# The sixteen batches of a cross attention: written out in line instead of a loop of two a turn

## The chip, the cores and the metric

The kernel runs on one core of a Trainium2 chip. The metric is the device time of one execution in microseconds, and a run is compared by its median. TensorE (PE), VectorE (DVE), ScalarE (ACT), GpSimd (POOL) and SyncE (SP) each run their own list of instructions; they meet only through semaphores.

## What is computed

A decoder layer on 16 batches of 100 tokens of width 128, in float32: a banded self attention, a cross attention with 16 heads over 1444 context rows per batch, and a mixture of 16 experts plus a shared part.

```python
x = x + _L0_attn_ref(_layernorm(x), WQ, WK, WV)
x = x + _L0_xattn_ref(_layernorm(x), ctx_1024, ctx_1024, mask, W_Q, b_Q, W_K, b_K, W_V, b_V, W_out, b_out)
x = x + _L0_ffn_ref(_layernorm(x), Wg, W1, b1, ...)
# _L0_xattn_ref, for each batch and head:
scores = jnp.einsum('bhqd,bhkd->bhqk', Q, K) / np.sqrt(D_K)
scores = jnp.where(attn_mask[:, None, :, :], -10000.0, scores)
attn = jax.nn.softmax(scores, axis=-1)
out = jnp.einsum('bhqk,bhkd->bhqd', attn, V)     # then @ W_out.T + b_out
```

## The kernel before

`decoder` runs three stages one after the other: `self_attention` (to about 112 us of the span), `cross_attention`, and `experts` (from about 1418 us). The cross attention is the subject. Weights are folded beforehand, so that a query row of a head is taken straight against the context, and products in float32 are made of three matmuls on operands split in a high and a low part (`_hi`, `_lo`).

A batch is one period of work. Its 1600 rows (100 tokens by 16 heads) are 12 tiles of 128 rows and one of 64. For each tile TensorE makes two halves of the scores (`score`, L1082), DVE adds the mask's bias and keeps the row's least (L997), ACT takes the exponential (L934), POOL normalizes by `row_inv` (L875, L877). TensorE then turns the rows (`turn`, transposes of L1098), ACT and DVE copy them out of PSUM as `pT_hi` (L943) and `pT_lo` (L1012), and TensorE multiplies them by the context (`values`, L1128), three steps behind the transposes. Each period also carries the preparation of the next batch (`prep`, context and queries) and, at 0.41 of its length, the projection of the batch before (`project`, L1171 to L1175), which DVE adds to the residual at L1059, once for each batch.

The order inside a period is a list, `ORDER`, worked out by `period()` on the host; each engine walks its own sorted form of it in `emit(b, odd)`. `odd` selects one of two sets of buffers, so two periods differ in buffers only. All engines share `periods`, which calls `emit` for -1, 0, 15 and 16 with a constant batch number, and for 1 to 14 in a loop of each engine, two batches a turn: seven turns, six jumps back. With a constant number every wait is against a constant, and one that is always met is left out; in the loop, `b` is in a register, each threshold is computed by the engine, and `wait_apart` adds a count on a semaphore of its own (`passed_sp`, `passed_pool`, `passed_dve`) behind the wait. `periods` is called in the blocks of all five engines. In the loop TensorE has 594 matmuls for each batch, and the other engines 140 (DVE), 86 (ACT) and 58 (POOL) instructions that do work.

Of the kernel before, what the change touches and what calls it, by code (L numbers as in the profile page):

```python
# [16 lines left out]
NB, S, D = 16, 100, 128  # L17
# [642 lines left out]
def cross_attention(nc, ctx_in, mask, banks, ident, A_hi, A_lo, VO, u, c_all,  # L660
# [3 lines left out]
    with ExitStack() as ctx:  # L664
# [84 lines left out]
        def periods(engine, emit):  # L749


            emit(-1, 1)
            emit(0, 0)
            with engine.Fori(1, NB - 2, 2) as b:
                emit(b, 1)
                emit(b + 1, 0)
            emit(NB - 1, 1)
            emit(NB, 0)

        with nc.Block() as block:  # L760
            @block.sync
            def _(sp):
# [37 lines left out]
                def emit(b, odd):  # L800
# [12 lines left out]
                    if here(b, 0) and here(b, 1):  # L813
# [3 lines left out]
                        load_x1(b + 1, 1 - odd)  # L817

                periods(sp, emit)
                sp.wait_ge(x2_stored, 16 * NB)  # L820

            @block.gpsimd
            def _(pool):
# [93 lines left out]

                start()
                periods(pool, emit)

            @block.scalar
            def _(act):
                order = act_order()

                def emit(b, odd):
                    for _, kind, db, j in order:
# [23 lines left out]
                        elif kind == "prep":  # L950
# [9 lines left out]
                            else:  # L960
# [3 lines left out]
                                act.copy(dst, qf[n % 2][:, :, :]).then_inc(prep_hi, 1)  # L964

                periods(act, emit)

            @block.vector
# [897 lines left out]
```

## Time and profile before

| | |
|---|---|
| median of 3 runs | 1603.62 us (1602.78 to 1609.25) |
| the profiled execution | 1606.2 us |
| its span, first to last instruction | 1604.5 us |
| busy: PE, DVE, POOL, ACT | 91%, 71%, 61%, 55% |
| mean granted clock of TensorE | 0.951 |
| matmuls | 10557 |
| first and last projection added (DVE L1059) | 240.12, 1415.71 us |

Busy shares are means over three unlike stages. "Idle before" in the timeline is the time an engine stood still ahead of a piece of work, and what ended it, as far as the semaphores show; "issue" means that nothing it waited for is seen. The granted clock is a share of TensorE's full speed.

### The profile page before, as it was taken

The numbers are of one execution on the slowest core, as the hardware profiler recorded it, in microseconds if no ns is written. First come the engines' busy times: TensorE is split into PE (matmuls) and PEld (weight loads), VectorE is DVE, ScalarE is ACT, GpSimd is POOL, SyncE is SP. The second block draws the span as 40 slices with busy tenths as digits, with TensorE's granted clock in tenths as the row PEclk, the third lists the DMA queues.
The fourth block names the chain that finished last, engine by engine and source line by source line (L and its number), as shares of the span: only waits on it lengthen the run. The fifth ranks groups of instructions, "written<-read, shape, count | busy, mean of one in ns | idle before, by whom it ended". The sixth has DMA issues, their size and how long they took to land. (4 is left out here: it accounts for less than half of the span.)

```text
span 1604.5 us, 35506 instructions
## 1 busy us (share of the span) xinstructions
PE 1463.2 (91%) x10557; PEld 1408.8 (88%) x10557; DVE 1143.5 (71%) x2672; ACT 883.8 (55%) x1632; POOL 973.1 (61%) x1101
## 2 busy tenths in 40 slices
PE   4856999999999999999999999999999999956796
PEld 4736999999999999999999999999999999945585
DVE  5644878686878687868686868686868686768565
ACT  0303656565656565656565656565656565625453
POOL 2015858575857585757675767576757585414564
PEclk9956999999999999999999999999999999966898
DMA  7021111111111111111110111011101011024422
GB/s 164 1 68 62 54 34 52 35 50 35 52 35 50 35 52 35 50 36 50 35 55 31 52 34 55 31 54 32 55 31 55 30 33 35 8 65 113 113 61 88
DMA packets 98038, 80.76 MB, mean 50 GB/s; under 512 B 17577, under 2 KB 96530, under 8 KB 97714
## 3 DMA queue, kind: packets, MB, share of 16 engines
q1 hardware_dynamic: 88848, 71.83, 15.1%
q10 hardware_dynamic: 6882, 2.21, 1.0%
q0 software_dynamic: 2112, 4.29, 0.8%
q8 instruction: 101, 1.65, 0.4%
q14 instruction: 95, 0.78, 0.1%
HBM read 67.26 MB, written 11.04 MB: 49 GB/s over the span
## 5 line engine op out<-in xcount | busy, mean ns | idle before, releaser
L943 ACT CAST pT_hi<-banks 128x512 fp32r<-128x512 f32 (+1 forms) x672 | 360.9, 542 | 342.6 <-PE banks L1098 337.5
L1012 DVE TENSOR_TENSOR pT_lo<-banks,pT_hi 128x512 fp32r<-128x512 f32 (+1 forms) x576 | 358.2, 626 | 220.3 <-ACT pT_hi L943 212.4
L875 POOL TENSOR_SCALAR probs<-probs,row_inv 128x1408 f32<-128x1408 f32 x192 | 278.7, 1451 | 235.7 <-DVE row_inv L1004 235.4
L1098 PE MATMUL banks<-ident,probs 128*128 128x128 f32 (+1 forms) x2304 | 365.8, 274 | 5.3 <-POOL probs_half L877 3.2
L1128 PE MATMUL banks<-pT_hi,ctx_hi 128*128 128x256 f32 (+1 forms) x1056 | 329.5, 312 | 17.8 <-DVE pT_lo L1012 13.8
L863 POOL TENSOR_SCALAR bias<-mask,c_cur 128x1444 f32<-128x1444 uint8 x192 | 282.9, 1473 | 82.4 <-DVE nmax L997 64.3
L934 ACT ACTIVATE probs<-probs,nmax 128x1448 f32<-128x1448 f32 x192 | 289.8, 1509 | 39.0 <-DVE nmax L997 38.9
L1128 PE MATMUL banks<-pT_hi,ctx_lo 128*128 128x256 f32 (+1 forms) x1056 | 303.1, 287 | 0.0
L1128 PE MATMUL banks<-pT_lo,ctx_hi 128*128 128x256 f32 (+1 forms) x1056 | 302.4, 286 | 0.0
L1098 PEld LDWEIGHTS banks<-ident,probs 128*128 128x128 f32 (+1 forms) x2304 | 271.0, 140 | 17.0 <-DVE pT_lo L1012 9.0
L1082 PE MATMUL banks<-ctxT_hi,qh 128*128 128x362 f32 x832 | 241.9, 372 | 4.8 <-POOL ql L912 2.8
L1128 PEld LDWEIGHTS banks<-pT_hi,ctx_hi 128*128 128x128 f32 x1056 | 201.1, 190 | 23.7 <-issue 16.0
L1082 PE MATMUL banks<-ctxT_lo,qh 128*128 128x362 f32 x832 | 208.2, 332 | 0.0
L1082 PE MATMUL banks<-ctxT_hi,ql 128*128 128x362 f32 x832 | 207.8, 331 | 0.0
L1128 PEld LDWEIGHTS banks<-pT_lo,ctx_hi 128*128 128x128 f32 x1056 | 200.8, 190 | 0.0
L1128 PEld LDWEIGHTS banks<-pT_hi,ctx_lo 128*128 128x128 f32 x1056 | 200.2, 190 | 0.0
L997 DVE CUSTOM_DVE_ANT_0 probs<-banks,bias,nmax 128x724 f32<-128x724 f32 x192 | 185.1, 964 | 4.6 <-PE banks L1082 3.9
L997 DVE CUSTOM_DVE_ANT_0 probs<-banks,bias 128x724 f32<-128x724 f32 x192 | 173.9, 906 | 12.8 <-PE banks L1082 7.6
L1082 PEld LDWEIGHTS banks<-ctxT_lo,qh 128*128 128x128 f32 x832 | 150.4, 192 | 0.0
L1082 PEld LDWEIGHTS banks<-ctxT_hi,ql 128*128 128x128 f32 x832 | 149.8, 191 | 0.0
L1082 PEld LDWEIGHTS banks<-ctxT_hi,qh 128*128 128x128 f32 x832 | 127.4, 193 | 8.0 <-DVE nmax L997 4.7
L964 ACT CAST qh<-qf 128x200 fp32r<-128x200 f32 x128 | 70.2, 548 | 104.7 <-DVE qf L1052 104.7
(287 smaller groups left out, 2339.9 us busy)
## 6 DMA issues: line engine op xcount, KB each, us to landing
mask<-in_mask_BxSxS_bk SPq DMA_DIRECT2D x192, 180.5 KB
nat<-in_ctx SPq DMA_DIRECT2D x16, 704.0 KB
up_raw<-in_L_ffn_W SPq DMA_DIRECT2D x32, 128.0 KB, 2.7
xs_dram<-empty SPq DMA_DIRECT2D x1, 2600.0 KB, 8.2
rows<-xs_dram SPq DMA_DIRECT2D x10, 260.0 KB, 3.0
down_raw<-in_L_ffn_W SPq DMA_DIRECT2D x16, 128.0 KB, 3.1
t_both<-yk_dram SPq DMA_DIRECT2D x3, 512.0 KB, 5.3
mask_half<-in_mask_BxSxS_bk SPq DMA_DIRECT2D x16, 90.2 KB
```

What stands on the lines that cost most here:

```text
L863: pool.tensor_scalar(bias[(t + i) % 2][0:n, 0:SK], src[:, :], MASKED, c_cur[i][0:n, t:t + 1], ALU.mult, ALU.add).then_inc(bias_ready, 1)
L875: pool.tensor_scalar(prob(j)[0:n, 0:FIRST], prob(j)[0:n, 0:FIRST], rinv[0:n, s:s + 1], 1.0, ALU.mult, ALU.mult)
L934: act.activation(prob(j)[0:n, 0:SKP], prob(j)[0:n, 0:SKP], ACT.Exp, bias=nmax[0:n, 1, s:s + 1], scale=-1.0, accum_out=rsum[0:n, s:s + 1]). ...
L943: act.copy(pT_hi[tslot(i, j)][:, 0:w], banks[:, T_BANK + j % 2, 0:w]).then_inc(turned_hi, 1)
L964: act.copy(dst, qf[n % 2][:, :, :]).then_inc(prep_hi, 1)
L997: dve.tensor_tensor_reduce(prob(t)[0:n, cs].rearrange("p (a k) -> p a k", a=2), src, bias[(t + i) % 2][0:n, cs].rearrange("p (a k) -> p a ...
L1012: dve.tensor_tensor(p_lo, turn, p_hi.bitcast(F32), ALU.subtract).then_inc(turned_lo, 1)
L1082: last = pe.matmul(banks[:, S_BANK + c, 0:CW], qpart[:, rows], kpart[:, c * CW:(c + 1) * CW], start=first, stop=qpart is ql[i])
L1098: last = pe.transpose(banks[0:m, T_BANK + j % 2, at_col:at_col + 128], prob(t)[:, c0:c0 + m], ident[:, :])
L1128: last = pe.matmul(banks[:, out_bank(g), 0:w], stationary[:, k, :], moving[tslot(i, j)][:, cs], start=(k == 0 and stationary is ctx_hi[i] ...
```

## The change

The six lines of `periods` become one loop on the host, which writes every batch out with a constant number. The same periods come in the same order with the same buffers: `b % 2` is 1 for -1 and 15 and 0 for 0 and 16, as in the calls it takes the place of.

```diff
@@ -749,13 +749,8 @@
         def periods(engine, emit):
 
 
-            emit(-1, 1)
-            emit(0, 0)
-            with engine.Fori(1, NB - 2, 2) as b:
-                emit(b, 1)
-                emit(b + 1, 0)
-            emit(NB - 1, 1)
-            emit(NB, 0)
+            for b in range(-1, NB + 1):
+                emit(b, b % 2)
 
         with nc.Block() as block:
             @block.sync
```

What follows from it in code that isn't edited: `known(b)` is now true for every batch, so `wait` and `wait_apart` take their constant form throughout, DMA sources are fixed slices in place of `bass.ds(b, 1)`, and the semaphores `passed_...` are never counted. Each engine's program holds sixteen periods where it held two and the four calls around them.

## Rows read from the trace of the kernel before

**Rows 1.** The page: span, busy time of the engines, TensorE's slices and granted clock.
```profile
span 1604.5 us, 35506 instructions
PE 1463.2 (91%) x10557; PEld 1408.8 (88%) x10557; DVE 1143.5 (71%) x2672; ACT 883.8 (55%) x1632; POOL 973.1 (61%) x1101
...
PE   4856999999999999999999999999999999956796
...
PEclk9956999999999999999999999999999999966898
```

**Rows 2.** The page: queues that carry only instructions.
```profile
q8 instruction: 101, 1.65, 0.4%
q14 instruction: 95, 0.78, 0.1%
```

**Rows 3.** Who waited for whom, TensorE: engine line waited for: us, times, longest.
```profile
PEld banks L1128 <- issue: 16.0, 7, 2.7
...
PE banks L1128 <- DVE pT_lo L1012: 13.8, 6, 2.4
```

**Rows 4.** Timeline 838.9 to 845.7: start, us, work [idle before <-releaser].
```profile
841.03 0.60 PE L1098 MATMUL banks<-ident,probs 128*128 128x128 f32 x4
...
842.52 0.68 DVE L1012 TENSOR_TENSOR pT_lo<-banks,pT_hi 128x512 fp32r<-128x512 f32 x1
...
842.82 1.47 POOL L863 TENSOR_SCALAR bias<-mask,c_cur 128x1444 f32<-128x1444 uint8 x1
843.99 0.19 PEld L1128 LDWEIGHTS banks<-pT_hi,ctx_hi 128*128 128x128 f32 x1 [2.59 <-issue]
844.00 0.38 PE L1128 MATMUL banks<-pT_hi,ctx_hi 128*128 128x256 f32 x1 [2.36 <-DVE pT_lo L1012]
...
845.47 0.42 DVE L1023 TENSOR_TENSOR oT_lo<-banks,oT_hi 128x256 fp32r<-128x256 f32 x1 [2.27 <-issue]
```

**Rows 5.** Busy time, stretches between projections: us, busy, clock, DMA.
```profile
core 0: us, PE busy (x) PEld busy (x) DVE busy (x) ACT busy (x) POOL busy (x), PEclk, DMA share, GB/s
318.52:399.91 81.39, 79.01 (x594) 77.76 (x594) 59.77 (x140) 48.46 (x86) 54.44 (x58) 0.98 0.14 43
...
478.34:559.96 81.62, 78.99 (x594) 77.76 (x594) 59.78 (x140) 48.47 (x86) 54.37 (x58) 0.98 0.14 42
559.96:638.35 78.39, 77.81 (x594) 76.41 (x594) 59.51 (x141) 48.33 (x86) 54.47 (x58) 1.00 0.14 43
638.35:718.49 80.14, 77.48 (x594) 76.25 (x594) 59.68 (x140) 48.49 (x86) 54.41 (x58) 1.00 0.14 43
718.49:796.88 78.39, 77.81 (x594) 76.39 (x594) 59.51 (x140) 48.36 (x86) 54.55 (x58) 1.00 0.14 44
796.88:878.51 81.63, 79.03 (x594) 77.79 (x594) 59.77 (x140) 48.48 (x86) 54.41 (x58) 0.98 0.14 42
...
1198.31:1276.68 78.37, 77.77 (x594) 76.36 (x594) 59.51 (x140) 48.33 (x86) 54.49 (x58) 1.00 0.14 43
1276.68:1354.66 77.98, 77.56 (x593) 76.19 (x593) 59.54 (x141) 48.34 (x86) 54.61 (x58) 1.00 0.10 33
```

**Rows 6.** The same view, the stretch after one stop.
```profile
844.31:847.72 3.41, 3.41 (x16) 3.41 (x15) 1.11 (x2) 0.58 (x1) 0.00 (x0) 0.50 0.20 59
```

**Rows 7.** Timeline of TensorE, two changes of batch without a jump.
```profile
1249.93 0.43 PE L1098 MATMUL banks<-ident,probs 128*128 128x128 f32 x2 [0.29 <-POOL probs_half L877]
...
1328.03 0.44 PE L1098 MATMUL banks<-ident,probs 128*128 128x128 f32 x2 [0.18 <-POOL probs_half L877]
```

**Rows 8.** Busy time, the same matmuls in line and in the loop.
```profile
178.83:204.41 25.58, 25.58 (x202) 25.55 (x202) 20.89 (x50) 17.51 (x30) 21.07 (x25) 1.00 0.18 54
335.55:361.08 25.53, 25.53 (x202) 25.53 (x202) 21.28 (x50) 17.49 (x30) 21.21 (x25) 1.00 0.19 55
```

**Rows 9.** Who waited for whom, POOL alone, 1320 to 1417 us.
```profile
POOL probs L875 <- DVE row_inv L1004: 18.4, 13, 3.6
POOL bias L863 <- DVE nmax L997: 12.1, 9, 2.1
```

## The prediction

> **What bounds the kernel now.** I read the page first. TensorE is busy for 91% of the span and its slices of the cross attention all stand at 9, while the next engine, DVE, has 71% [rows 1]. So only what makes TensorE wait there, or run slower, can move the end. Busy tenths are too coarse for a stop of 2 us in a slice of 40 us, so the next view is who waits for whom. Two entries stand out: the weight loads of L1128 waited for "issue", that is for nothing the profile shows, 16.0 us in 7 waits, and the matmuls of L1128 waited 13.8 us in 6, which the view puts down to DVE's pT_lo [rows 3]. The loop runs `b` over 1, 3, ... 13: seven turns, six jumps back. Six stops fit that.
>
> The timeline around one of them (839 to 845 us) says what they are. TensorE starts the last transposes of a turn at 841.03 and its next weight load at 843.99, after 2.59 us of idle on "issue"; the matmul behind it is named as waiting 2.36 us for DVE's pT_lo, but the piece of pT_lo that is on the way there began at 842.52 and took 0.68 us, so it was over at 843.20, 0.8 us before. DVE has a stop of its own on "issue", 2.27 us, up to 845.47; POOL goes on at 842.82 as if nothing were [rows 4]. No other engine is late, no transfer is named: the engines that stop are short of instructions. I take this as the jump back to code that the engine no longer has at hand. The page fits: queues that carry only instructions fetch 1.65 MB in 101 packets and 0.78 MB in 95 [rows 2]; a loop held on the engine would not need a fetch every 16 us to the end.
>
> Last I cut the span at the projections (DVE L1059, one for each batch, 16 in all), which gives one interval for each batch. An interval with a jump in it takes 80.14 to 81.63 us, one without takes 78.4, with the same 594 matmuls in both [rows 5]. That is the price list of this prediction.
>
> **What the change removes.** Six jumps back. The six intervals are 81.39, 81.62, 80.14, 81.63, 81.63 and 81.39 us, together 487.80 (the last two, from 956.88 and 1116.92, repeat the fourth and the first and are not shown). Six clean ones at 78.39 (mean of the seven mid-loop intervals, of which three stand in the rows and none is over 0.05 away) are 470.34. Difference: 17.46 us. These are net prices, since both kinds of interval end in the same place of the schedule, so waits that a stop happened to cover are already subtracted.
>
> The price has two parts. The interval from 638.35 keeps its clock at 1.00 and costs 80.14 - 78.39 = 1.75 us: the bare stop. The other five have a granted clock of 0.98 and cost 3.00 to 3.24 [rows 5]. In the one I looked into, the loss is a single stretch of 3.41 us at 0.50, the lower level (1.2 GHz), starting 0.3 us after TensorE resumes [rows 6]; ahead of it the engine had stood for over 2 us. Work that streams at half rate for 3.41 us loses 1.7 us, of which some hides small waits. So the six stops cost 6 x 1.75 = 10.5 us and the five slow stretches 17.46 - 10.5 = 7.0 us. Without a stop nothing else in these intervals lowers the clock: the clean ones all show 1.00. I count both as gained.
>
> Here a rule of the Trainium skill speaks against the change: "Advanced Engine Details and Errata", Control Flow Timing, gives a compare-and-branch about 108 ns. By that six jumps would be worth 6 x 0.108 = 0.65 us, an estimate from that page. The trace disagrees with it for this loop: 1.75 us net at the least [rows 5].
>
> **What it adds and moves.** No operation, transfer or buffer is added, removed or reordered on any engine; batches 0 and 15 already ran in line with constant numbers, now 1 to 14 do as well. Waits against a computed value, the arithmetic for it and the extra semaphore counts of `wait_apart` go. Is that worth anything on TensorE, the engine that counts? Two bounds. In the middle of a batch, no: 25.58 us for 202 matmuls of batch 0 in line (178.83 on) against 25.53 for the same 202 in the loop (335.55 on) [rows 8], so 0, or a loss of 0.05. At the change of batch, a little: the last interval, which crosses out of the loop into in-line code without a jump, takes 77.98 us against 78.39 [rows 5], 0.41 less, and the wait for POOL's probs_half there is 0.18 us instead of 0.29 [rows 7]. It is one instance, and batch 15 has no next batch to load, which may be part of it. For 13 changes of batch the bounds are -0.7 and +5.3 us. I take half of the upper one's 0.41, 0.2 us each, because the crossing itself (shorter waits) is what all 13 share and the missing loads are not: 2.6 us. Both ends stay in the range.
>
> What TensorE stopped for is also cover for others. If it goes, who is late next? In a clean change of batch TensorE waits only 0.18 to 0.29 us for probs_half [rows 7], and three intervals in a row (559.96 to 796.88) ran at full clock with a single stop [rows 5]; DVE and POOL keep up. DVE's own pause at the jump vanishes with TensorE's.
>
> In-line code has to be fetched throughout. TensorE does that already: some five fetches of 16 KB in each clean interval of 78.4 us (101 over the span [rows 2]), none visible as a stop. The page of the skill "Runtime: NRT & Kernel Launch", Instruction fetch mechanics, says why: fetching ahead works in sequence, and only a taken jump out of the window waits for the fetch. What carries the number is the row: 0 us. POOL and SyncE are the new case. POOL does not stop at the jump [rows 4], so its loop code seems to stay at hand, and now it will be fetched. In the in-line stretch from 1320 to 1417 us POOL's waits of any length are for row_inv and nmax, none on "issue" [rows 9]. I cost it at 0, cover being its idle time (POOL 61% busy [rows 1]).
>
> **Sum.** 17.46 + 2.6 = 20.1 us. The profiled execution took 1606.2 us (span 1604.5, 1.7 around it): 1586.1. The median of the runs is 1603.62, 2.6 below it, and the sum is absolute, so the forecast is 1603.6 - 20.1 = 1583.5 us.
>
> **Rivals.**
> 1. *Full clock is not granted for so long.* The engine would run from 145 to some 1400 us with no pause; the longest stretch at 1.00 in the rows is the 237 us from 559.96 to 796.88, with one stop in it. If the chip takes a 3.41 us stretch at 0.50 about as often as now (one in each 160 us of two intervals, eight in 1270 us), 8 x 1.7 = 13.6 us come back: 1597.1. For it: five of six turns have one. Against: each stands right behind a stop, and none stands in a clean interval [rows 5, 6]. Chance 0.06.
> 2. *Slower: POOL, now fetching, stops once in each batch.* Place: POOL L875/L877, whose normed rows TensorE waits for at the change of batch. Price by the nearest row, DVE's stop of 2.27 us at the jump [rows 4]: 14 x 2.27 = 31.8, so 1583.5 + 31.8 = 1615.3. It turns the sign once more than 20.1 / 14 = 1.4 us per batch reaches TensorE. For: POOL, with only 58 working instructions a batch, is the engine whose loop was most likely held without fetches. Against: no such wait in line [rows 9], and idle time in front of most of its operations. Chance 0.04.
> 3. *The change does nothing.* The stops belong to something else with a period of two batches (a transfer, the masks) and stay, or a jump is next to free: 1603.6, or 1601.0 with the shorter changes of batch. By the skill's 108 ns above this is the outcome. Against: the mid-loop change of batch does the same work and has no stop, the crossing out of the loop has none either [rows 5, 7]. Chance 0.04.
> 4. *Half the gain:* the stops shrink but stay at half their price, since the fetches that they wait for may lag in-line code too: 1603.6 - 17.46 / 2 - 2.6 = 1592.3. Chance 0.04.
>
> **Chances.** Forecast 0.82, rivals 0.06, 0.04, 0.04, 0.04. Own range of the forecast: gain 16.8 (17.46 - 0.7) to 22.8, plus 1.7 either way for how the slow stretch behind the cross attention falls on the shorter schedule, plus the scatter of the runs of before, whose median stands 0.8 above the lowest and 5.6 below the highest: 1578.5 to 1590. Up to 1592 most of rival 4's neighbourhood comes in; rivals 1 to 3 stay out, 0.14, and some of the forecast's tails. About 0.5%, 8 us, is what a measurement of this kernel can tell from no change. Faster by more: 0.88 (forecast, rival 4, a part of what lies near). Same: 0.08 (rivals 1 and 3, less their tails). Slower: 0.04 (rival 2).
>
> **What would show it.** In the profile after: no waits on "issue" of over 2 us at L1128, nor at DVE L1023; 15 intervals of projections of which the first 14 all lie between 77.9 and 78.5 us; granted clock 1.00 in every one. Instruction packets of the large queue stay near 101, the small queue's rise, since POOL and SyncE now fetch too. Clean intervals at 78.0 to 78.2 would show the change-of-batch term right, 78.4 wrong. I am wrong if stretches at 0.50 appear inside clean intervals (rival 1), if POOL gets waits on "issue" and TensorE longer ones for probs_half or pT_lo (rival 2), or if the stop of TensorE stays each 160 us (rival 3).

## The result and the profile after

| | before | after |
|---|---|---|
| median | 1603.61 us (4 runs, 1602.78 to 1609.25) | 1585.47 us (4 runs, 1580.95 to 1587.76) |
| the profiled execution | 1606.2 us | 1583.9 us |
| its span | 1604.5 us | 1581.9 us |
| mean granted clock | 0.951 | 0.958 |
| from the first projection to the fifteenth | 1114.5 us | 1094.7 us |

The ratio is 0.9876, with a 95% interval of 0.9843 to 0.9909: 18.1 us less, where 20.1 were forecast. A second set of six runs of the same kernel gave 1585.57 us, with 1604.16 for before. (Before has one run more than the table ahead of the prediction.) An execution can also fall into a slower state as a whole, which happened to two of the ten runs of one kernel below, all engines but TensorE in the loop, its profiled one among them: its median is that of the other eight, and of its profile only the intervals between projections are read.

The last row of the table is the yardstick of all that follows. Runs of one kernel spread by some us ahead of and behind the cross attention, but the fourteen intervals between the first fifteen projections repeat: 1094.7 us here, 1095.0 in the second set's profile. "The 14 intervals" below are this stretch, from one profiled execution of each kernel.

The page after. The columns of the first two lines are as in [rows 1], those of the queues as in [rows 2]:

```profile
span 1581.9 us, 29748 instructions
PE 1452.9 (92%) x10557; PEld 1400.0 (88%) x10557; DVE 1136.0 (72%) x2672; ACT 883.4 (56%) x1632; POOL 972.7 (61%) x1101
...
PEclk9966999999999999999999999999999999967898
...
q8 instruction: 85, 1.39, 0.4%
q14 instruction: 61, 0.50, 0.1%
```

The same work (10557 matmuls, 2672 instructions of DVE), but 5758 instructions fewer in all, nearly all of them the arithmetic of the computed waits: by the trace 5378 on registers, 345 on semaphores and 35 branches. It shows in the fetches too, 85 packets for 101 and 61 for 95.

TensorE's weight loads in who waited for whom, against [rows 3]:

```profile
PEld banks L1123 <- issue: 9.2, 15, 0.8
PEld banks L1093 <- POOL probs_half L872: 7.9, 16, 0.7
```

The waits of 2.4 to 2.7 us at the loop's jumps are gone; the longest on "issue" at this line is 0.8 us. What is left belongs to the change of batch: sixteen waits for probs_half.

Busy time between projections (the columns are those of [rows 5]). The first three shown, the second, fourth and sixth interval, held a jump before; the last is the fourteenth, which was in part in line already:

```profile
317.50:395.65 78.15, 77.57 (x594) 76.29 (x593) 59.08 (x140) 48.36 (x86) 54.57 (x58) 1.00 0.14 43
...
473.85:552.05 78.20, 77.58 (x594) 76.31 (x593) 59.07 (x140) 48.38 (x86) 54.59 (x58) 1.00 0.14 44
...
630.37:708.53 78.16, 77.58 (x594) 76.30 (x593) 59.18 (x141) 48.35 (x86) 54.52 (x58) 1.00 0.15 44
...
1255.75:1333.97 78.22, 77.57 (x594) 76.29 (x593) 59.18 (x140) 48.43 (x86) 54.62 (x58) 1.00 0.11 32
sum 1094.68, PE 1086.09 PEld 1068.68 DVE 827.43 ACT 677.20 POOL 763.25; mean PE 77.58 PEld 76.33 DVE 59.10 ACT 48.37 POOL 54.52
```

All fourteen lie between 78.15 and 78.32 us, at a granted clock of 1.00.

### The profile page after: what moved, and what is told of

It is laid out like the page before. It is cut to its first block and busy times, and to the rows that moved or that the text cites. A ratio compares the mean times of both kernels' runs of the same rounds, so it can differ in the third digit from the quotient of the medians.

```text
span 1581.9 us, 29748 instructions
## 1 busy us (share of the span) xinstructions
PE 1452.9 (92%) x10557; PEld 1400.0 (88%) x10557; DVE 1136.0 (72%) x2672; ACT 883.4 (56%) x1632; POOL 972.7 (61%) x1101
## 5 line engine op out<-in xcount | busy, mean ns | idle before, releaser
L858 POOL TENSOR_SCALAR bias<-mask,c_cur 128x1444 f32<-128x1444 uint8 x192 | 282.9, 1474 | 81.1 <-DVE nmax L992 68.2
```

The source lines that it names most:

```text
L858: pool.tensor_scalar(bias[(t + i) % 2][0:n, 0:SK], src[:, :], MASKED, c_cur[i][0:n, t:t + 1], ALU.mult, ALU.add).then_inc(bias_ready, 1)
```

## The experiments

The theory: the engine has to fetch the instructions that a jump back leads to and stands still for it, and the pause of TensorE brings the slow clock stretch behind it. Rivals: the jump itself is dear; the computed waits are; the stops of the other engines are what counts.

**The loop with its jump announced.** One change to the kernel before: the loop is built so that each engine is told at the top of a turn which instructions the jump will need.

```diff
-            with engine.Fori(1, NB - 2, 2) as b:
+            with nc.Fori(1, NB - 2, 2, engines=[engine.engine], hint_back_edge=True) as b:
```

> The kernel before with its loop of two batches a turn, and one addition: at the top of each turn every engine is told which instructions the jump at its end will need, so that they can be fetched ahead. The jump, the loop and the computed waits stay. My theory (the stop is the late fetch of the loop's first instructions, and the slow clock stretch is its consequence): the intervals with a jump fall from 80.1 to 81.6 us to those without, 78.4 us, six times 2.9 us, so 17.5 us less than before, about 1586 us. Rival (a jump costs what it costs, wherever its target lies): no change, 1603.6 us. Rival (computed waits and the registers are the price): no change either, 1603.6 us. Telling mark: granted clock 1.00 in all intervals and no wait of over 2 us on issue at TensorE.

Median 1589.38 us (4 runs; before 1610.82 in 19 runs beside it, ratio 0.9843, interval 0.977 to 0.9917). The 14 intervals take 1096.2 us, 1.5 more than in the kernel after and 18.3 less than in the kernel before. Busy time between projections, the first with a jump, the second without:

```profile
317.64:395.92 78.28, 77.68 (x594) 76.25 (x594) 59.66 (x141) 48.38 (x86) 54.56 (x58) 1.00 0.14 43
395.92:474.27 78.35, 77.78 (x594) 76.35 (x594) 59.48 (x140) 48.38 (x86) 54.63 (x58) 1.00 0.14 43
```

The loop, its six jumps and its computed waits are all there (35541 instructions, before 35506; the 35 more are one announcement for each engine and turn), and 92% of what writing it out gains is had. The jump as such and the waits are not the price.

That it is the fetch, the trace shows. In the kernel before TensorE's fourth jump holds its sequencer (the part of an engine that reads the list) from 839.45 to 843.58 us, and the one 16 KB instruction packet of that time starts at 841.27 and ends at 842.22. It is so at all six jumps: the packet starts 1.3 to 1.9 us after the jump has begun, and the jump ends 1.4 us after the packet. With the jumps announced, they last 0.35 to 0.50 us and none has a packet in it. (A packet 3.4 to 5.5 us ahead of the jump stands in both runs, so which one brings the target is not shown.) The queue's line for 839.45 to 843.58 before:

```profile
q8 instruction: 1, 0.02, 1.4%
```

**Who has to be in line.** The loop of the kernel before is kept for some engines, the others run in line:

```diff
-        def periods(engine, emit):
+        def periods(engine, emit, loop=False):
+            if loop:
+                ...   # emit(-1), emit(0), the loop, emit(NB - 1), emit(NB)
+                return
             for b in range(-1, NB + 1):
                 emit(b, b % 2)
```

TensorE in line, the four others in the loop:

> TensorE's list written out in line, the other four engines in the loop of two batches. My theory: TensorE's own stop was the price, so most of the gain is there. DVE and ACT still stop for about 2.3 us at each jump, and TensorE waits for their copies with only one step of about 2 us as cover, so I expect 0.5 to 1.5 us of each of six stops to come through: 1586 + 3 to 9 = 1589 to 1595 us. Rival (the stops of DVE and ACT are the bound and TensorE's is hidden behind them): 1600 us or more. If nothing comes through: 1586 us.

TensorE in the loop, the four others in line:

> The mirror of the run above: TensorE alone keeps the loop of two batches, the other four engines are in line. My theory: six stops of TensorE with five or six slow clock stretches stay, 17.5 us over the kernel after, 1602 to 1604 us. Rival (the other engines' stops or their computed waits cost the time): 1586 to 1589 us.

ACT alone in the loop, then DVE alone:

> ACT alone keeps the loop of two batches, the four other engines are in line. With all four in the loop and TensorE in line the intervals with a jump took 79.6 to 79.8 us. If ACT's late fetch is what came through (it makes pT_hi and the exponential of the last rows), the intervals with a jump take 79.3 to 79.8 us here; if it is DVE's, they take 78.2 to 78.4.

> DVE alone keeps the loop of two batches. ACT alone in the loop lengthened the intervals with a jump to 79.3 to 79.6 us, which is all that the four engines together did with TensorE in line. If DVE's stop of over 2 us is hidden behind the cover of TensorE's lag, as that leaves room for: 78.2 to 78.6 us; if DVE's stop is as dear as ACT's and the two only overlap: 79.3 to 79.8 us.

| in the loop | intervals with a jump | the 14 intervals | more than after |
|---|---|---|---|
| all (before) | 80.14 to 81.63 | 1114.5 | 19.8 |
| all but TensorE | 79.6 to 79.8, one 81.7 | 1107.7 | 13.0 |
| TensorE alone | 79.2 to 79.8, two at 81.1 and 81.3 | 1106.3 | 11.6 |
| ACT alone | 79.3 to 79.6 | 1102.8 | 8.1 |
| DVE alone | 79.1 to 79.3 | 1101.5 | 6.8 |
| none (after) | 78.15 to 78.32 | 1094.7 | |

Medians, in the order of the four rows below the first: 1603.5 us (8 runs), 1608.73 (10), 1592.48 (8) and 1594.29 (one run), where before measured beside them had 1610.82, 1610.82, 1605.6 and 1604.16. The ratios to before are 0.9943 (0.9897 to 0.9989), 0.9969 (0.9926 to 1.0013) and 0.9908 (0.9884 to 0.9933). In the first two sets the runs spread over 17 to 22 us, so the total alone would not tell TensorE alone in the loop from before; these readings rest on the intervals.

With TensorE in line and the others not, 13.0 of the 19.8 us stay, more than the 3 to 9 that I expected. 1.9 of the 13.0 are a slow clock stretch in the interval of 81.7, behind a pause of 1.7 us that brought none in the five others; without it about 11 stay. The mirror run refutes its expectation too: TensorE alone in the loop costs 11.6 us more than after, not 17.5, with two slow stretches instead of five. Busy time of such an interval, then who TensorE waited for in the same run; the last fence is who waited for whom in the run with DVE alone in the loop, where DVE's stop on "issue" is that of [rows 4] again:

```profile
490.64:570.47 79.83, 77.90 (x594) 76.32 (x594) 59.58 (x140) 48.47 (x86) 54.44 (x58) 1.00 0.14 43
```

```profile
PE banks L1101 <- POOL probs_half L880: 12.2, 16, 1.5
```

```profile
PE banks L1101 <- POOL probs_half L880: 10.7, 16, 1.4
...
DVE oT_lo L1026 <- issue: 13.2, 6, 2.3
```

In the kernel after, TensorE waits 4.7 us for probs_half in 16 waits, at most 0.5 at a time. ACT's stop is not on "issue" in the views, but the trace has it: in the kernel before, the first instruction of the next turn comes 2.4 to 2.7 us after ACT's jump and 2.7 to 2.9 us after DVE's, with the jump announced 0.2 and 0.5 us after; POOL's and SyncE's come 0.2 us after in both. A stop of DVE or ACT at the change of batch delays the last tile on its way through exponential, reciprocal and norm, and TensorE stands for it. I had DVE's stop hidden, or as dear as ACT's; at 0.8 to 1.0 us over its own clean intervals (78.3) it is neither, but nearer the second. So the stops overlap: TensorE's alone costs 1.0 to 1.5 us at full clock, ACT's alone 1.1 to 1.3, DVE's alone 0.8 to 1.0, all of them together 1.75. Each of the three has to be mended to have the gain; mending TensorE's alone gave 6.9 of 19.8 us, or 8.8 without the slow stretch of that profile.

**The computed waits.** Batches 1 to 14 stand out in a loop of a single turn:

```diff
-            for b in range(-1, NB + 1):
-                emit(b, b % 2)
+            emit(-1, 1)
+            emit(0, 0)
+            with engine.Fori(1, 2, NB - 2) as b:
+                for n in range(NB - 2):
+                    emit(b + n, 1 - n % 2)
+            emit(NB - 1, 1)
+            emit(NB, 0)
```

> Batches 1 to 14 stand out in line inside a loop of a single turn, on all engines: no jump back is ever taken, but the batch number is in a register and every wait, address and extra count is computed as in the kernel before. My theory: only the shorter change of batch is lost, 13 times 0.2 us, so about 2.6 us over the kernel after: 1588 us, intervals at 78.4 us and clock 1.00 throughout. Rival (the computed waits carry the price): 1600 to 1604 us.

1585.78 us (4 runs), the 14 intervals 1095.0 us. This looks like a refutation of my 2.6 us for the waits, but the page says it is none:

```profile
span 1584.1 us, 29763 instructions
```

The kernel after has 29748, before 35506: the computed waits are not in the program that ran, most likely because the number of a single turn is a constant. The run says nothing about the waits. The nearest rows are the run with the announced jump, with all waits computed and no stop. Its seven intervals without a jump take 78.36 us in the mean; in the kernel before they take 78.39, in the kernel after 78.20 and in its second profile 78.25. There computed waits cost 0.11 to 0.16 us a batch, the greater part of the 0.2 that I had put down for the change of batch. Its six with a jump take 78.29, 0.12 more than after.

**Fewer jumps, longer body.** Three turns of four batches, the first two batches in line:

```diff
-            for b in range(-1, NB + 1):
+            for b in range(-1, 3):
                 emit(b, b % 2)
+            with engine.Fori(3, 12, 4) as b:
+                for n in range(4):
+                    emit(b + n, 1 - n % 2)
+            emit(NB - 1, 1)
+            emit(NB, 0)
```

> Loop of four batches a turn on all engines (batches 3 to 14 in three turns, the rest in line): two jumps back instead of six, and one longer body. My theory (a price for each jump, whatever its body's length): two intervals of 80.1 to 81.6 us, all others 78.1 to 78.4, so 2 x 2.9 + 10 x 0.2 = 7.8 us over the kernel after: 1593 us. Rival (a price for the looped batches, by computed waits): 12 of 14 batches stay looped, so 1600 us.

Median 1589.96 us (4 runs; before 1605.6 beside it, ratio 0.9893, interval 0.9836 to 0.9949). The 14 intervals take 1100.9 us, 6.2 more than in the kernel after (7.8 expected). Two of them are long, 80.03 and 81.42, the others 78.0 to 78.5:

```profile
630.62:710.65 80.03, 77.58 (x595) 76.35 (x594) 59.66 (x141) 48.46 (x86) 54.49 (x58) 1.00 0.14 44
945.48:1026.90 81.42, 79.11 (x595) 77.88 (x594) 59.74 (x141) 48.45 (x86) 54.56 (x58) 0.98 0.15 43
```

The price goes by jumps taken, not by the number of batches in the loop: 1.8 and 3.1 us over their neighbours.

**A pause without a jump.** Is the slow clock stretch the pause's or the jump's? In line throughout, TensorE's list gets waits that are met long before, at six changes of batch (in the trace two of them make one instruction):

```diff
             for b in range(-1, NB + 1):
+                if b in range(3, NB - 2, 2):      # on TensorE alone
+                    for _ in range(pauses):       # 70, in the second run 84
+                        engine.wait_ge(zeroed, 7)
                 emit(b, b % 2)
```

> The kernel after, all in line, with 70 waits on a semaphore long since met put into TensorE's list at six changes of batch (ahead of batches 3, 5, 7, 9, 11 and 13). They keep TensorE's sequencer for some 50 to 100 ns each, 3.5 to 7 us, with no jump, no fetch out of order and no computed value; TensorE has about 2 us of matmuls queued, so its array should stand for 1.5 to 5 us. My theory (the slow clock stretch is a consequence of the pause): the six intervals lengthen by the pause less 0.6 us, and most show a granted clock of 0.98 with a stretch at 0.50 behind the pause, another 1.2 to 1.5 us each. Rival (the slow stretch belongs to the jump or its fetch): granted clock 1.00 in all intervals.

> As the run with 70 met waits, which stopped TensorE for 1.9 to 2.0 us at each of six places with the clock at 1.00 throughout, but with 84, which should stop it for 2.6 to 2.8 us, as long as the jumps of the kernel before did. No jump and no late fetch. My theory (the pause alone brings the slow stretch): at least three of the six pauses are followed by a stretch at 0.50, and those intervals take 81.0 to 81.7 us, the others 80.0 to 80.3. Rival (the jump's fetch is needed for it): six intervals at 80.0 to 80.3 and the clock at 1.00.

Medians 1593.98 (8 runs) and 1601.63 us (one run). Who waited for whom, TensorE's weight loads, 70 and 84 waits:

```profile
PEld banks L1125 <- issue: 20.3, 21, 1.9
```

```profile
PEld banks L1125 <- issue: 24.9, 21, 2.7
```

Two intervals of the first and four of the second (its last two, 81.75 and 81.77, repeat the third):

```profile
316.36:395.69 79.33, 77.42 (x594) 76.26 (x593) 59.03 (x140) 48.44 (x86) 54.43 (x58) 1.00 0.14 42
473.88:553.31 79.43, 77.40 (x594) 76.25 (x593) 59.04 (x141) 48.41 (x86) 54.49 (x58) 1.00 0.14 43
```

```profile
317.37:397.48 80.11, 77.42 (x594) 76.24 (x593) 59.05 (x141) 48.47 (x86) 54.49 (x58) 1.00 0.14 42
475.69:557.36 81.67, 78.98 (x594) 77.84 (x593) 59.15 (x141) 48.44 (x86) 54.48 (x58) 0.98 0.14 42
635.71:717.49 81.78, 78.96 (x594) 77.79 (x593) 59.23 (x140) 48.42 (x86) 54.49 (x58) 0.98 0.14 42
795.72:875.83 80.11, 77.42 (x594) 76.26 (x593) 59.05 (x141) 48.45 (x86) 54.41 (x58) 1.00 0.14 42
```

The second run makes the kernel before again without any jump: 1113.0 us for the 14 intervals against 1114.5, four intervals of 81.7 to 81.8 with a clock of 0.98 and two of 80.1 with 1.00. The pause alone brings the slow stretch. In the first, none of six pauses of 1.8 to 1.9 us did: my expectation of "most" was wrong. A pause costs less than it lasts. The matmuls stand 1.6 to 1.7 us, and the interval is 1.2 us longer; of the difference, 0.3 us is TensorE's wait for probs_half, which is gone at these six changes of batch (8 such waits in the 14 intervals, after 14). Where the rest is saved was not looked into.

**A jump to what is at hand.** At the same six places, a loop of one met wait:

```diff
             for b in range(-1, NB + 1):
+                if b in range(3, NB - 2, 2):      # on TensorE alone
+                    with engine.Fori(0, 21, 1):
+                        engine.wait_ge(zeroed, 7)
                 emit(b, b % 2)
```

> The kernel after, all in line, with a small loop on TensorE alone at the same six changes of batch: 21 turns of one met wait, so 20 jumps back to a target three or four instructions away. My theory (only a jump to instructions that are no longer held is dear): 0.1 to 0.3 us for each turn, 2 to 6 us for a place, less 2 us that is queued: the six intervals grow by 0 to 4 us. Rival (any jump back costs 2 us or more): 20 of them are over 40 us for each place, and the six intervals take about 120 us.

1629.18 us (2 runs; ratio to before 1.0135, 1.0062 to 1.0208). The six intervals take 85.5 us, 7.3 more than in the kernel after; the weight loads pause for 5.8 us in each, and the clock falls to 0.50 for 6.8 us:

```profile
317.02:402.47 85.45, 79.59 (x594) 78.44 (x593) 59.13 (x140) 48.44 (x86) 54.62 (x58) 0.96 0.13 40
```

Add the 2 us that were queued and divide by 21 turns: 0.37 us for each, with the wait and the counting in it (in the trace the branches stand 0.36 to 0.47 us apart). That is above the 0.1 to 0.3 expected, and 7.3 us is above the 0 to 4. The rival of 2 us or more for any jump, intervals of about 120 us, is out. The branch itself, which the views leave out, stands in the trace with 0.21 us where it is taken to code at hand, against 3.9 to 4.2 us at the six jumps of the kernel before; TensorE's queued matmuls covered some 2 us of those. The Trainium skill's figure weighed in the prediction, 108 ns for a compare-and-branch ("Advanced Engine Details and Errata", Control Flow Timing), is half of a near jump's 0.21 us here and says nothing of a far one. That a taken branch out of what is held waits for a fetch, as the Trainium skill has it in "Runtime: NRT & Kernel Launch", Instruction fetch mechanics, agrees with the packet inside each of the six jumps.

**What is left at the change of batch.** Timeline of the kernel after, DVE, ACT and POOL on the way of the last tile, then TensorE:

```profile
1068.62 0.19 ACT L929 ACTIVATION_READ_ACCUMULATOR probs_half<-probs_half,nmax 64x1 f32 x1
```

```profile
1069.92 0.90 DVE L992 CUSTOM_DVE_ANT_0 probs<-banks,bias 128x724 f32<-128x724 f32 x1
...
1070.75 0.15 DVE L999 RECIPROCAL row_inv<-row_sum 64x1 f32<-64x1 f32 x1
```

```profile
1070.99 1.44 POOL L870 TENSOR_SCALAR probs_half<-probs_half,row_inv 64x1408 f32<-64x1408 f32 x1 [2.16 <-DVE row_inv L999]
```

```profile
1072.82 0.44 PE L1093 MATMUL banks<-ident,probs 128*128 128x128 f32 x2 [0.29 <-POOL probs_half L872]
```

The sums are there at 1068.8, but DVE takes the reciprocal only at 1070.75, behind a half score of the next batch; POOL idles 2.16 us and TensorE waits. One instruction is moved:

```diff
             if j % 2:
-                out.append((n + 3.6, "recip", db, j // 2))
+                out.append((n + (3.6 if j // 2 < FT else 2.9), "recip", db, j // 2))
```

> The kernel after, unchanged, as the measure for early_recip on the same chip and for the median of the result. Expected 1581 to 1588 us, intervals between projections at 78.15 to 78.3 us, clock 1.00 in them.

> The kernel after with one instruction moved on DVE: the reciprocal of the last tile's sums (row_inv of probs_half) goes ahead of the first half score of the next batch, 0.83 us of work, instead of behind it. What is left between clean intervals and matmuls alone is the wait of TensorE for probs_half, 0.4 to 0.5 us at each of 15 changes of batch. My theory: POOL can start 0.8 us earlier, the wait goes, the half score starts 0.1 us later and nobody waits for that: intervals of 77.8 us, 5 to 6 us less in all, about 1580 us. Rival (TensorE is then held at the next wait in the same place, or the score is late): same as the kernel after.

The kernel after again: 1585.57 us (6 runs). With the reciprocal moved: 1578.15 us (7 runs), ratio to before 0.9827 (0.98 to 0.9855). The 14 intervals take 1088.2 us, 6.8 less than the 1095.0 of the kernel after measured beside it (5 to 6 expected), and no wait of TensorE for probs_half is left in them:

```profile
795.23:872.88 77.65, 77.32 (x594) 76.30 (x593) 58.95 (x140) 48.41 (x86) 54.56 (x58) 1.00 0.14 43
```

It is the fastest version of the study: 26.0 us, 1.6%, under the 1604.16 of before measured beside it (11 runs). The profiled execution was the longest of the seven, 1588.33 us; its first projection comes 12 us later than in the kernel after, and behind that its intervals are the shortest of all.

## Why the prediction was right, point by point

- **The stops are the jumps back, and the fetch behind them.** Right, and shown: announced jumps stop nobody, and the instruction packet that stands inside each of TensorE's jumps before is gone from them.
- **17.46 us for six of them, as net prices between like intervals.** Right. The six intervals that took 487.80 us take 469.0 now; of the 18.8 us between, 17.5 are the stops and the rest is the next term.
- **Its parts, 10.5 us of pauses and 7.0 of slow clock.** Right in kind: a pause of the same length without a jump gives both prices, 80.1 and 81.7.
- **0.2 us for each of 13 changes of batch.** The size was right, 78.19 against 78.39 us in the mean. That was luck: the row it leaned on did not carry it. The last interval, 77.98 us in part in line before [rows 5], is 78.22 wholly in line, no shorter than the others, and the half that I took of its 0.41 us was a choice, not a reading. So the 14 intervals gained 17.46 + 13 x 0.20 - 0.24 = 19.8 us. Why the mixed interval was shorter is open. What the 0.2 us is made of, the intervals without a jump tell in part: 0.11 to 0.16 is the computed waits, by the run with announced jumps.
- **Who is late next.** "DVE's own pause vanishes with TensorE's" held, but I did not price it, and ACT's I did not see: "No other engine is late" was wrong, ACT's list stood for 2.4 to 2.7 us behind its jump. The sum was not hurt, because it took net prices and the change mends all engines at once. It is no detail even so: had only TensorE been written out, over half of the loss (11 to 13 of 19.8 us) would have stayed. In the timeline of [rows 4] TensorE's stop overlaps theirs. The rival in which the stops belong to something else is out with the announced jumps.
- **Fetching in line costs nothing, POOL's included.** Right. POOL has no wait on "issue" between 145 and 1396 us of the profile after; its waits there are for row_inv, nmax and qh alone. The rival with POOL is out. So is that of stops that shrink by half: no pause of TensorE of over 1 us is left in the 14 intervals. But the sign of the packets was wrong: I expected about 101 and more than 95, it was 85 and 61. I had counted the code that is newly fetched, and forgotten both the 5758 instructions that go and what each jump fetched again: one packet of the large queue inside each jump of TensorE, and one or two of 8 KB within 1.2 us of a jump of DVE or ACT.
- **Full clock for so long.** The rival is out: 1.00 in all fourteen intervals, 1095 us, with no pause of over 1 us. The rows had 237 us at 1.00 as the longest stretch; the trace before has 314 already, from 530.28 to 844.31 us. There is no slow stretch at times of its own; where one stands in the cross attention of any run, a pause came before it or it began inside one.
- **The total.** The spans of the profiled executions differ by 22.6 us, 19.8 of it in the 14 intervals, 0.8 ahead of them and 1.9 behind the last projection, where nothing was changed. The medians differ by 18.1. Both profiles stand off their medians, before 2.6 above, after 1.6 below; the forecast's sum, 20.1, is nearer to the 19.8 of the stretch itself than to either total. The range does not add up as it stands: its terms give 1578.3 and, with all 5.6 us of the scatter above the median, 1594 at the upper end, where I wrote 1590. The 1585.47 lies inside either.

## What to carry to other kernels

A long loop turn can pay for every jump back, on each engine by itself: here turns of 402 instructions and more did, turns of 265 and fewer did not. Cut the span at a piece of work that recurs once a turn, and compare the intervals with and without the jump, since that gives the net price at once. Write the body out, or announce the jump, on all engines that stop, not on the busiest alone. Then look at what is left in the same place: here a reciprocal queued behind 0.8 us of other work, worth 6.8 us once the stops were gone (in the loop it was not tried).

## What the runs showed of the hardware

- A taken jump of TensorE held its sequencer for 0.21 us to code at hand, 0.35 to 0.5 us to far code that had been announced, and 3.4 to 4.2 us to far code that had not. The last held one instruction packet of 16 KB, which took 0.9 to 1.5 us.
- A turn of the loop is 2601 instructions on TensorE, 591 on DVE and 402 on ACT, counted in the trace, and these stop at the jump. POOL with 265 and SyncE with 190 do not: their next turn's first instruction comes 0.2 to 0.3 us after it, DVE's and ACT's 2.4 to 2.9 us. Where between 265 and 402 it begins, and whether that is the same on all engines, was not tried.
- TensorE's pauses at the changes of batch (by its weight loads) and its granted clock, over all profiles: of 20 pauses of 1.4 to 2.0 us none was followed by a stretch at 0.50 (with all engines but TensorE in the loop 1 of 6 at 1.7 us was), of 17 of 2.3 to 2.7 us 11 were, and one of 2.1 us; each stretch lasted 3.4 us and began up to 1.4 us after the work resumed. Length is not all: a pause of 1.7 us at 149 to 161 us, ahead of the 14 intervals and 4 to 5 us after the clock had risen to 1.00, stands in all 14 profiles and was followed by such a stretch within 0.6 us in four. With pauses of 5.8 us the clock fell inside the pause, six times of six, for 6.8 us. Why some of the pauses between bring it and others of the same length do not, these runs do not tell.
